# Layer 1's attention of a two-layer decoder: query projections placed between the half batches instead of behind the last

## What is computed

```python
q = hidden_states @ Wq.T                                   # 16 heads of 128
k = hidden_states @ Wk_down.T @ Wk_up.T + k_anchor          # 4 heads of 128
v = hidden_states @ Wv_down.T @ Wv_up.T + v_anchor          # 4 heads of 128
...
q = q * cos + _rotate_half(q) * sin
k = k * cos + _rotate_half(k) * sin
...
scores = jnp.einsum('bhqd,bhkd->bhqk', q, k) * scaling      # causal mask, softmax
out = jnp.einsum('bhqk,bhkd->bhqd', attn, v)
...
return out @ Wo.T
```

## Time and profile before

| | us |
|---|---|
| median of 3 runs | 1871.56 (1869.31 to 1871.92) |
| the profiled execution, time | 1871.72 |
| the profiled execution, span from first to last instruction | 1869.9 |
| layer 1's attention with its projections, about | 1276 to 1595 on the span's clock |

### The profile page before, as it was taken

One profiled execution on the slowest core, in us unless ns is written; L12 is line 12 of the kernel. 1 busy time (PEld: TensorE's weight loads), 2 busy tenths in 40 slices (PEclk: granted clock), 3 DMA queues, 4 the chain that ended last, 5 costly groups with the idle time before them and its releaser, 6 DMA issues.

```text
span 1869.9 us, 29060 instructions
## 1 busy us (share of the span) xinstructions
PE 1792.0 (96%) x11730; PEld 1179.7 (63%) x11730; DVE 998.8 (53%) x1892; ACT 606.0 (32%) x1931; POOL 409.6 (22%) x488
## 2 busy tenths in 40 slices
PE   7999999999999999999889999998999999999998
PEld 6766666646665665666555888876577674444444
DVE  4765666426666666557644111116645455565887
ACT  1233222315555565555640111110312213232511
POOL 2432323512020220120003000006121020002476
PEclk9999999999999999999998999999999999999999
DMA  9100002000000000000214988965000021643011
GB/s 377 42 1 1 1 1 107 1 15 18 18 18 15 4 18 18 1 17 2 113 69 174 368 331 327 339 254 198 27 1 1 1 107 50 250 161 124 3 38 40
DMA packets 31109, 170.62 MB, mean 91 GB/s; under 512 B 3865, under 2 KB 3865, under 8 KB 17185
## 3 DMA queue, kind: packets, MB, share of 16 engines
q1 hardware_dynamic: 28416, 161.43, 22.9%
q0 software_dynamic: 2560, 7.34, 1.3%
HBM read 155.91 MB, written 16.52 MB: 92 GB/s over the span
## 4 chain that ended last, share of the span: by engine, by line
PE 83%; DVE 9%; POOL 4%; ACT 2%; issue 2%; DMA 1%; SPq 0%; POOLq 0%; DVEq 0%
PE PS L1142 8%; PE PS L985 6%; PE PS L1222 6%; PE PS L936 6%; PE PS L1019 5%; PE PS L1058 4%; PE PS L1010 4%; PE PS L1286 4%; PE PS L1182 4%; PE PS L1151 4%; PE PS L1255 3%; PE PS L1042 3%; PE PS L1273 3%; PE PS L1078 2%; PE PS L993 2%
## 5 line engine op out<-in xcount | busy, mean ns | idle before, releaser
L2046 POOL TENSOR_TENSOR rstd<-veps,mhalf 112x1 f32<-112x1 f32 (+1 forms) x76 | 58.0, 764 | 577.2 <-DVE veps L1315 554.0
L1142 PEld LDWEIGHTS PS<-R,W 128*128 128x128 f32 x1344 | 155.8, 195 | 11.8 <-issue 11.8
L1142 PE MATMUL PS<-R,W 128*128 128x128 f32 x1344 | 156.2, 278 | 2.2 <-DVE R L1610 2.2
L1439 DVE TENSOR_REDUCE nmx<-PS 112x2 f32<-112x750 f32 x128 | 114.0, 931 | 81.4 <-PE PS L1042 81.4
L1910 ACT ACTIVATE R<-PS,nmx 112x375 f32<-112x375 f32 x256 | 142.9, 573 | 3.7 <-DVE nmx L1439 3.7
L936 PE MATMUL PS<-xT,W 128*128 128x224 f32 x640 | 127.1, 359 | 1.1 <-DMA W<-in_w0kv 0.8
L936 PEld LDWEIGHTS PS<-xT,W 128*128 128x128 f32 x640 | 123.0, 194 | 7.7 <-issue 5.5
L1617 DVE TENSOR_TENSOR R<-R,PS 128x512 f32<-128x512 f32 x21 | 14.5, 688 | 201.7 <-PE PS L1142 201.7
L1387 DVE TENSOR_TENSOR x<-x,PS 112x512 f32<-112x512 f32 x40 | 27.5, 687 | 170.0 <-PE PS L985 82.4
L1255 PE MATMUL PS<-W 128*128 128x512 f32 x256 | 117.6, 602 | 0.0
L985 PE MATMUL PS<-W,R 128*112 128x512 f32 x256 | 113.7, 597 | 0.0
(11 more groups left out here) (291 smaller groups left out, 3233.7 us busy)
## 6 DMA issues: line engine op xcount, KB each, us to landing
W<-in_we SPq DMA_DIRECT2D x63, 1024.0 KB, 8.3
W<-in_entwT SPq DMA_DIRECT2D x8, 1024.0 KB, 7.3
W<-in_entpw SPq DMA_DIRECT2D x8, 1024.0 KB, 8.5
W<-in_ctxT SPq DMA_DIRECT2D x8, 750.0 KB, 4.2
R<-in_ctxT SPq DMA_DIRECT2D x8, 750.0 KB, 8.4
R<-in_ctx SPq DMA_DIRECT2D x8, 750.0 KB
xs_rows<-in_x SPq DMA_DIRECT2D x3, 1792.0 KB, 38.2
R<-xs_rows SPq DMA_DIRECT2D x21, 256.0 KB, 9.1
```

The source lines that it names most:

```text
L1142: o = e.matmul(PS[:, m, c * 128:(c + 1) * 128], gate_up(j % 3, k, off + c * 128), BT[:, j % 2, k, :], start=k == 0, stop=k == 3)
L1439: e.tensor_reduce(nmx[0:S, par, r:r + 2], PS[0:S, r:r + 2, 0:SC], AX.X, ALU.max, negate=True).then_inc(*up("cmax", (b, c, par, r)))
```

## The change

One entry is added to the table of costs:

```diff
 COST = {"turn": 0.45, ...
-        "td": 1.5, "ku": 0.8, "vp1": 0.9, "s1": 2.6, ...
+        "td": 1.5, "ku": 0.8, "vp1": 0.9, "kq1": 3.0, "s1": 2.6, ...
```

## The result

| | before | after |
|---|---|---|
| median of the runs made side by side, us | 1870.02 (20 runs, 1866.07 to 1871.92) | 1872.85 (20 runs, 1869.69 to 1875.21) |
| span of the profiled execution, us | 1869.9 | 1870.9 |
| mean granted clock in it | 0.984 | 0.985 |
| the stage, us (defined below) | 263.23 | 266.32 |

The two medians differ by 2.8 us. The ratio worked out from all the runs is 1.0017, with an interval of 1.0010 to 1.0024. That makes 3.2 us slower (1.9 to 4.5), inside the 0.2% that I called no difference. The forecast was 1873.9, 2.3 us above the 1871.56 of before.

A forecast was written before the change was run, and what follows sets the result against it. PE was taken as the bound, saturated in units 0 to 2. A removed wait of 0.27 us and added stalls of 2.6 us gave +2.3 us, 1873.9 us for the median, range 1870.8 to 1877.4.

The forecast's parts named there:

- The bound: Units 0 to 2: PE is busy for all but 0.06 of 127 us, so almost no idle time to take.
- The turns' wait: First gap of units 0 and 1: second turn waits for the second key's bank, 1.2 us each (0.9 to 1.4).
- The query's bank in unit 0: Behind the turns in unit 0's first gap: a query projection waits for the first vp1's bank, another 0.18 us.
- the one removed from the old lump: Start of unit 0's old query lump: the first query projection's wait for its bank goes, gain 0.27 us.
- The boundaries: Between kinds of step, 11 places with work put in before and after: cost 0, bounds 0.3 us either side.
- The sum: Whole kernel: -0.27 + 2.6 = +2.3 us, 1873.9 us for the median, counted as no difference.
- A: First gaps of units 0 and 1: the stall is hidden, time 1871.3 us; chance 0.14.
- B: First gaps of units 0 and 1: the clock falls, 1877.4 us with one fall, 1880.8 with two; chance 0.06.
- C: First gaps of units 0 to 2: late c1 in DVE's queue is paid, 0.9 us each, 1876.6 us; chance 0.06.
- D: Whole plan: not two by two, queries go 1, 4, 3 and 3, 2, 3, small steps affected more; no chance given.

The follow-up runs named there:

- the turns first: Kernel after with the two turns ahead of the keys in the first gap of units 0 and 1; 1871.77 us, 1.0009 of before.
- the gathering alone: Kernel after with each unit's eight queries back in one lump, small steps still drawn together; stage 269.27 us, 267.57 less the clock's fall.
- the start alone: Kernel before with unit 1's two td ahead of unit 0's half batches 0 and 1, nothing changed behind unit 3; 1868.51 us, 1.0001.
- the kernel that mixes kinds: Kernel before with 14 steps in one gap, by kind in unit 1, alternating in unit 2; these rows take 31.16 and 31.61 us.
- the first try at the start: Kernel before with both td of unit 1 ahead of unit 0's first s1, both its vp1 ahead of the second; 1871.21 us, 1.0010.

## Why the prediction was right, and where it was not

**The bound.** That PE is saturated in units 0 to 2 held: of 132 us from 1400 on it is busy for 132.00, as before.

**The turns' wait.** Computed 1.11 us, taken as 1.2, measured 1.11 in both units. The wait that the prediction named, on the line and for the instruction that it named, came to the hundredth, start to start. The adding of 0.1 "if the gap of the six steps is made up from the half batches" was wrong: the plain chain of the rows was the better number. That the cause is the single scratch area was a reading; the experiment with the second one shows it.

**The query's bank in unit 0.** Computed 0.18, measured 0.22 from start to start; the one removed from the old lump was of the same size, and together they are about zero. Little of the 0.22 is the bank's: in unit 1, where an `s1` with banks of its own follows, the step behind the second turn starts 0.54 us after it, and here 0.60. What the wait costs besides is in the query itself, 3.29 us instead of 3.03.

**The boundaries.** This is the step that failed: "a boundary between kinds of step costs nothing that I can see", 0 with bounds of 0.3 us. Measured: 0.87 us, of which the stalls may have up to 0.1. The prediction looked at one boundary, the `s1` behind a query and behind a `td`, both 1.76, and concluded for all. The answer was in its own working: it has the six small steps of the earlier trace rows at 6.83 us in a row, and never set against them what they take where they lie spread, 6.41 us in unit 2 of the same trace. In after the six take 6.95. In before's rows the `s1` behind a `ku` starts before the last matmul of the `ku` has ended; in after's rows for the six in a row no step starts like that:

```profile
1492.59 1.59 PE L1168 MATMUL PS<-R,W 64*128 64x224 f32 x7
1493.84 0.35 PE L1195 MATMUL PS<-R 64*112 64x112 f32 x1
1494.02 0.35 PE L1168 MATMUL PS<-R,W 64*128 64x224 f32 x1
1494.02 1.92 PE L1195 MATMUL PS<-R 64*112 64x112 f32 x31
```

(Timeline of before, unit 2: an `s1` row between two rows of `ku`.) That bears on the `ku` alone, a third of the loss in unit 2; why `td` and `vp1` are longer in a row stays open. The term should have been worked out by adding the steps' durations in both orders.

**The sum.** 2.2 + 0.87 = 3.1 in the stage, 3.2 in the runs; predicted 2.3. Both are within 0.2%. The miss of 0.8 us is the boundaries; the stated range, 1870.8 to 1877.4, is wide enough not to show it.

**The rivals.** A fell: neither stall is hidden. B fell: two stalls of 1.11 us did not bring the clock down. The Trainium skill, TensorE: Matmul & The Clock Gate, section on a second failure mode, tells of a clock that oscillates where PE micro-idles frequently between groups of matmuls; the two idle spots here, 66 us apart, left it at 1.00 in the stretches above. C fell, twice over: no wait for L1657 in units 0 to 2 of after, and none beyond the usual 0.19 us even with no cover; its `c1` was 0.6 us late, not 0.9. D held in full. The queries went 1, 4, 3 and 3, 2, 3 and cost nothing; 2.2 of the 3.1 us belong to the turns behind the keys, 0.9 to the small steps in a row.

**Why spreading the queries does not pay here.** The Trainium skill, Perfetto Trace Analysis, section Optimization Strategy, says that interleaving may help where the most-contended engine changes from one regime to the next. Here it is PE in the half batches and in the lump alike, so that is no case of it, and the two kernels that spread the queries with the small steps left alone are 1.24 and 1.6 us longer in the stage.

## What to carry to other kernels

Before spreading work over gaps, add up the idle time of the bounding engine in them: where it is near zero there is nothing to win, and an order can lose, by new meetings of steps that share a bank and by steps that take up to 0.2 us more behind another kind of step. A new entry in a planner's cost table moves everything that the planner places, so write out both orders and cost the steps that did not carry the new number too. Where a moved step takes a bank from a step whose reader works through a single scratch area, count that reader's chain from the rows; here it came out to 0.01 us.

## What the runs showed of the hardware that I had not expected

**Matmuls of other shapes in a row.** A query projection takes 3.03 us behind its like, a `vp1` or the second `td`, and 3.23 behind a `ku` or the first `td`, with the same instructions and no wait.

**A second stretch of half clock that comes and goes.** In unit 3, PE waits 1.95 us ahead of the last `p1`. In six of the profiles (the turns first, two scratch areas, the gathering alone, both kernels with the queries split and the small steps as before, and the start alone) the clock falls behind that wait: these windows are of the kernel with two scratch areas,

```profile
1570.00:1578.00 8.00, 6.05 (x21) 2.95 (x20) 3.67 (x5) 2.53 (x11) 0.00 (x0) 0.96 0.32 133
1578.00:1586.00 8.00, 8.00 (x18) 3.34 (x17) 4.29 (x3) 0.10 (x1) 0.00 (x0) 0.83 0.02 10
```

and its `w1` there takes 8.17 us instead of 6.87. In both profiles of before, both of after, the kernel that mixes kinds and the first try at the start it does not fall, with the same order of instructions and the same wait. It is worth 1.7 us and hides a difference of the size studied here, and why it comes in some I could not settle. A third such place lies some 115 us ahead of the end, at the end of a wait of 1.9 us. The granted clock over 5 us there is 0.66 to 0.68 in nine of the fourteen profiles, among them the second of after, and 1.00 in the other five, among them the first. There the same kernel takes 281.86 us from the last `w1` to the end with the fall and 281.62 without.

**Time goes with the mean clock, in steps.** Runs of before at a mean clock of 0.987 took 1866.2 to 1867.2 us, at 0.985 1868.1 to 1870.9. Some kernels that move work in this stage have a lower mean (0.9822 to 0.9838), and the change itself does not (0.9856 and 0.9852).
